# Matmuls on constants in TensorE's waits, in a twelve-layer perceiver kernel

## What is computed

```python
x = x + _L0_xattn_ref(_layernorm(x), ctx_768, ...)   # one head
x = x + _L0_attn_ref(_layernorm(x), ...)             # 16 heads, causal, latent projection
x = x + _L0_ffn_ref(_layernorm(x), ...)              # 8 experts, each picks its top 16 tokens
x = x + _L1_xattn_ref(_layernorm(x), ctx_768, ...)   # 16 heads of 64
x = x + _L1_attn_ref(_layernorm(x), ...)             # 16 heads of 16 + 32
x = x + _L1_ffn_ref(_layernorm(x), ...)              # 16 experts, top 2, capacity 8
x = x + _L2_xattn_ref(_layernorm(x), ctx_768, ...)   # 16 heads of 64
x = x + _L2_attn_ref(_layernorm(x), ...)             # one head, causal
x = x + _L2_ffn_ref(_layernorm(x), ...)              # 8 experts, masks by affinity and rank
x = x + _L3_xattn_ref(_layernorm(x), ctx_768, ...)   # one head
x = x + _L3_attn_ref(_layernorm(x), ...)             # one head
x = x + _L3_ffn_ref(_layernorm(x), ...)              # 64 small two-layer networks
```

```python
aff = num / (x_norm * w_norm[None, None, :] + 1e-09)
cap = jnp.floor(S * jax.nn.sigmoid(aff.mean() - affinity_threshold)).astype(jnp.int32)
...
ranks = jnp.argsort(jnp.argsort(-aff, axis=1), axis=1)
dispatch = tcr * (ranks < cap)
```

## Time and profile before

| | |
|---|---|
| median of 3 runs | 1697.69 us (1694.96 to 1699.32) |
| the profiled execution | 1698.85 us, span 1697.1 us |
| mean granted TensorE clock | 0.881 |
| TensorE matmul busy | 1439.9 us, 85% of the span, 9148 records |
| VectorE, ScalarE, GpSimd busy | 877.0, 644.0, 115.8 us |
| share of the last chain | TensorE 74%, VectorE 14% |

### The profile page before, as it was taken

One profiled execution on the slowest core, in us unless ns is written; L12 is line 12 of the kernel. 1 busy time (PEld: TensorE's weight loads), 2 busy tenths in 40 slices (PEclk: granted clock), 3 DMA queues, 4 the chain that ended last, 5 costly groups with the idle time before them and its releaser, 6 DMA issues.

```text
span 1697.1 us, 22614 instructions
## 1 busy us (share of the span) xinstructions
PE 1439.9 (85%) x9148; PEld 886.4 (52%) x9148; DVE 877.0 (52%) x1631; ACT 644.0 (38%) x890; POOL 115.8 (7%) x76
## 2 busy tenths in 40 slices
PE   5967578899999998786889999999846788886975
PEld 3556367355555556564845555555532555554543
DVE  5545421466566552434246566565266766664434
ACT  4502011355555551110135555555112556453202
POOL 0000000000000000000000000000030434230000
PEclk9975589899999999785789999999965999897985
DMA  5210126255565665001225565556400232230000
GB/s 198 79 50 1 49 99 248 35 107 102 107 106 100 105 109 171 1 0 75 100 44 100 106 106 100 106 106 110 121 25 25 77 103 95 87 126 11 1 0 13
DMA packets 283976, 140.22 MB, mean 83 GB/s; under 512 B 271840, under 2 KB 271840, under 8 KB 277472
## 3 DMA queue, kind: packets, MB, share of 16 engines
q1 hardware_dynamic: 283872, 138.77, 34.0%
HBM read 71.10 MB, written 0.52 MB: 42 GB/s over the span
## 4 chain that ended last, share of the span: by engine, by line
PE 74%; DVE 14%; issue 6%; ACT 3%; POOL 2%; DMA 1%; POOLq 0%; SPq 0%; ACTq 0%; DVEq 0%; PEldq 0%; PEld 0%
PE ps L226 28%; PE ps L1595 5%; PE ps L1559 4%; PE ps L1581 4%; PE ps L1598 3%; PE ps L1582 3%; PE ps L1583 3%; PE ps L1561 3%; PE ps L1560 3%; PE ps L1562 3%; PE ps L1566 2%; PE ps L1522 2%; PE ps L1542 2%; PE ps L1613 2%; PE ps L1619 2%
## 5 line engine op out<-in xcount | busy, mean ns | idle before, releaser
L885 DVE TENSOR_REDUCE wk<-ps 128x1 f32<-128x1024 f32 x128 | 156.8, 1225 | 233.0 <-PE ps L1566 233.0
L545 ACT ACTIVATE wk<-ps,wk 128x1024 f32<-128x1024 f32 x128 | 142.7, 1115 | 237.9 <-DVE wk L885 237.9
L226 PE MATMUL ps<-ring,wk 128*128 128x256 f16 (+2 forms) x1032 | 169.4, 318 | 36.8 <-DVE wk L1411 32.1
L226 PE MATMUL ps<-wk,ring 128*128 128x512 f16 (+4 forms) x896 | 188.2, 364 | 9.7 <-ACT wk L710 2.4
L226 PEld LDWEIGHTS ps<-ring,wk 128*128 128x128 f16 (+2 forms) x1032 | 126.8, 129 | 81.5 <-DVE wk L1411 38.7
L554 ACT ACTIVATE wk<-wk 128x1024 f16<-128x1024 f32 x128 | 146.9, 1148 | 53.6 <-DVE wk L892 53.6
L900 DVE SCALAR_TENSOR_TENSOR wk<-wk 128x1024 f16<-128x1024 f32 x128 | 163.4, 1277 | 2.4 <-ACT wk L554 2.4
L226 PEld LDWEIGHTS ps<-wk,ring 128*128 128x128 f32 (+1 forms) x896 | 110.4, 167 | 64.7 <-issue 26.3
L226 PE MATMUL ps<-wk 16*64 16x64 f32 (+7 forms) x1012 | 89.5, 287 | 25.4 <-DVE wk L1372 11.1
L463 POOL TENSOR_TENSOR rstd<-rstd,cst 128x4 f32<-128x4 f32 x13 | 13.1, 1010 | 1372.4 <-DVE rstd L841 1372.4
L1559 PE MATMUL ps<-ctx_T,ring 128*128 128x512 f16 x256 | 97.7, 382 | 3.6 <-DVE ring L881 3.0
(11 more groups left out here) (293 smaller groups left out, 2322.4 us busy)
## 6 DMA issues: line engine op xcount, KB each, us to landing
ring<-units SPq DMA_DIRECT2D x50, 1024.0 KB, 5.7
ring<-context SPq DMA_DIRECT2D x16, 384.0 KB, 3.9
wk<-context SPq DMA_DIRECT2D x16, 384.0 KB, 3.2
ring<-wk SPq DMA_TRANSPOSE x120, 3.1
ring<-units SPq DMA_DIRECT2D x2, 768.0 KB, 6.5
xn<-wk SPq DMA_TRANSPOSE x64, 3.1
xnT<-wk SPq DMA_TRANSPOSE x64, 3.1
cst<-consts SPq DMA_DIRECT2D x1, 912.5 KB, 5.2
```

Of the source, the lines that this page charges most:

```text
L226: return PE.matmul(out, lhsT, rhs, start=start, stop=stop)
L545: ACTE.activation(WXP[:, t % 2, :], bank(2 * (t % 2), 1024), ACT.Exp, bias=WNM[:, t % 4:t % 4 + 1], accum_out=WRS[:, t % 4:t % 4 + 1]).the ...
L885: DVE.tensor_reduce(WNM[:, t % 4:t % 4 + 1], bank(2 * (t % 2), 1024), X, ALU.max, negate=True).then_inc(xa_max, 1)
```

## The change

A helper `keep_clock(n, b)` on TensorE issues `n` matmuls of fp16 operands, 128 x 128 weights and 512 columns, both read from `cst`, into bank `b`, which nothing reads at that time. It waits for nothing and tells nothing. It is called ahead of every layernorm's transposes, in `self16` ahead of each tile's wait for `sa_P` (12 for the first tile of a half, 5 for the others), in `self1` ahead of the wait for `s1_P`, and at ten places in the routers and in the last layer. In `self16` the wait for `sa_vs` moves from behind the first tile's transposes to ahead of its fillers. There are 522 such matmuls in one execution.

```diff
+            def keep_clock(n, b):
+
+                for _ in range(n):
+                    PE.matmul(ps[:, b, :], cst[:, 0:64].bitcast(F16), cst[:, 0:256].bitcast(F16), start=True, stop=True)
+
-            def layernorm(key):
+            def layernorm(key, spare=7, n=8):
+                keep_clock(n, spare)
                 for i in range(NT):
                     pe.wait_ge(ln_xn, 4 * LN[key] + i + 1)
...
                     def attend(u):
                         t = 8 * k + 4 * h + u
                         ii, j = u // 2, u % 2
+                        if u == 0:
+                            pe.wait_ge(sa_vs, 2 * k + h + 1)
+                        keep_clock(12 if u == 0 else 5, 7)
                         pe.wait_ge(sa_P, t + 1)
...
                         pe.wait_ge(sa_PT, t + 1)
-                        if u == 0:
-                            pe.wait_ge(sa_vs, 2 * k + h + 1)
...
                 ins.then_inc(s1_S, 1)
+                keep_clock(16, 1)
                 pe.wait_ge(s1_P, 1 + k)
...
-            layernorm(0)
+            layernorm(0, n=18)
...
             ins.then_inc(router_logits, 1)
+            keep_clock(8, 7)
             pe.wait_ge(router_d, 1)
             spread_scores(0)
+            keep_clock(44, 7)
             pe.wait_ge(L0f_sel, 1)
...
             ins.then_inc(comb_T, 1)
+            keep_clock(8, 4)
             pe.wait_ge(xin_copied, 4)
...
-            layernorm(3)
+            layernorm(3, n=24)
...
             ins.then_inc(router_logits, 1)
+            keep_clock(14, 7)
             pe.wait_ge(L1f_hot, 1)
...
             mm(bank(3, 64, at=64), C("same"), TU, False, True).then_inc(L1f_cum, 1)
+            keep_clock(16, 7)
             pe.wait_ge(L1f_disp, 1)
...
-            layernorm(6)
+            layernorm(6, spare=2)
...
-            layernorm(8)
+            layernorm(8, spare=3)
...
             ins.then_inc(router_logits, 1)
+            keep_clock(56, 7)
             pe.wait_ge(L2f_sums, 1)
...
             mm(bank(3, 2, at=8), C("ones"), RB_[:, 0:2]).then_inc(L2f_summed, 1)
+            keep_clock(10, 7)
             pe.wait_ge(L2f_mean, 1)
...
+            keep_clock(40, 7)
             pe.wait_ge(L2f_xnl, 1)
             gather(0)
...
-            layernorm("9b")
+            layernorm("9b", n=36)
...
-            layernorm(11)
+            layernorm(11, spare=3)
...
             ins.then_inc(L3f_s, 1)
+            keep_clock(36, 7)
             pe.wait_ge(L3f_acc, 16)
```

## The result

The changed kernel takes 1691.44 us (median of 20 runs, 1669.84 to 1707.87), the one before 1697.28 (20 runs, 1694.37 to 1699.32): 5.8 us less by these medians. The ratio, 0.9928 with the interval 0.9906 to 0.9950, says 12.2 us, because it leaves out the seven slow executions of the changed kernel, those more than 1.5% above its fastest; the median of the other 13 is 1685.99. So 6 to 12 us are gained where 29 were forecast; the time lies inside the range, near its upper end. The profiled execution took 1687.22, span 1685.4, against 1697.1 before: 11.7 us.

A forecast was written before the change was run, and what follows sets the result against it. TensorE's speed, 1.2 instead of 2.4 GHz in low stretches, was taken as the bound. Terms 9 + 14.5 + 6 + 7 + 5 + 1 - 12.3 = 30 us gave 1698.85 - 30 - 1.2 = 1668 us, range 1646 to 1693.

The forecast's parts named there:

- the 56: Third router: 56 fillers ahead of four small matmuls that start a chain push the rest of the program, -12.3 us.
- (c): Rival at the third router: the 56 fillers are hidden, 1656 us; chance 0.06.
- (f): Rival: matmuls on constants don't hold the clock, nothing gained, the 56 cost 24 and the loops 22: 1744 us; chance 0.03.
- The layernorms' share: Layernorms with 8 fillers: 13.0 us saved at full clock, times 0.7, gives 9.
- I take 0.8 and 0.2: Multi-head self-attention half-loops: 0.8 for full clock, 0.2 for low; loops 5 us, with the stages behind 14.5.
- three signs of being wrong: Loops run low (round over 7 us), clock falls after most layernorms, or L1339 no longer waits for GpSimd.
- the first single-head attention with its layernorm: Single-head self-attentions: 16 fillers in a 4.55 us gap, 6.4 times 0.9 gives 6 us; layernorms counted in their 9.
- the last layer: Last layer: 36 fillers in 9.75 us, then eight matmul pairs, half of 4.4 taken; 5 us with the other long gaps.
- One more, for a stretch of expert matmuls that by chance fell low: 1: Expert matmuls: 1 us gained for a stretch that by chance fell to the low clock.
- (a): Likeliest case: clock mostly up in self-attentions, part of the layernorms, the 56 paid: 1648 to 1690 us; chance 0.60.
- (d): Rival: idle left behind fillers, with transposes and copies, still drops the clock at most layernorms: 1680 us; chance 0.12.
- (e): Rival: fillers at the low clock in the multi-head loops, 5.4 us lost per half, 22 in all: 1704; chance 0.09.

The follow-up runs named there:

- e3: Kernel before plus only the 108 fillers of the multi-head self-attentions and the moved wait for sa_vs: 1685.31 us, ratio 0.9936.
- e6: Kernel before plus only the 150 fillers ahead of layernorms: 1681.02 us, ratio 0.9915.
- e4: Kernel before plus only the 56 fillers of the third router: 1710.29 us, ratio 1.0079.
- e1: Changed kernel with the 56 fillers moved behind the first two small matmuls of the third router: 1677.43 us, ratio 0.9878.
- e9: e5 plus 3 fillers in each copy wait of the multi-head loops, between a tile's transposes and its value matmuls: 1659.30 us, ratio 0.9784.
- e7: e3 with fillers that read 16 rows instead of 128, same columns: 1719.64 us, ratio 1.0137.
- e14: A further profile of the changed kernel, nothing edited: 1689.32 us, one run.
- e5: Changed kernel plus 8 and 3 fillers ahead of and within the second feed-forward's experts: 1670.75 us, ratio 0.9849.
- e8: Changed kernel with e1's and e5's edits, 11 fillers per layernorm, 3 in copy waits of layernorms and self-attentions: 1643.71 us, ratio 0.9690.
- e12: e8 plus 3 fillers each in score-spreading waits and ahead of the last cross-attention's and single-head output projections: 1638.69 us, ratio 0.9655.
- e2: Changed kernel without the 108 fillers of the two multi-head self-attentions: 1708.69 us, ratio 1.0072.
- e11: Changed kernel without the 56 fillers: 1680.74 us, ratio 0.9880.
- e10: Kernel before plus only the 8 and 3 fillers at the second feed-forward's experts: 1692.06 us, ratio 0.9965.
- e15: Another further profile of the changed kernel, nothing edited: 1676.46 us, one run.

## Why the prediction was right, and where it was wrong

**The direction and most mechanisms were right.** Matmuls on constants hold the clock (e3, e6); rounds at the full clock are 4.55 us; the 56 push the rest by their whole length, +12.98 us at VectorE's step behind the four small matmuls against the 12.3 forecast, and alone they cost 13.1 (e4). The gap behind them stayed, and moving them gave 14 (e1). Rivals (c) and (f) are out. The layernorms' share up to the first loop came as forecast only on average (3.2 forecast, 4.4 in this execution, 1.5 to 6.3 over four); the second router gave 2.2 as forecast, the first 3.2 for 2.4.

**The step that failed is "I take 0.8 and 0.2"**, the chance of a half-loop being at the full clock, which made 14.5 us of the multi-head attentions. The prices on both sides of it were sound: 24.8 us when all four are up (e9, forecast 25.1), 20.3 lost when all are down and stay so (e7, forecast 22, with nothing gained behind). But in the change 5 of the 16 half-loops of four executions ran at the full clock throughout, none of them in the second attention. There the clock fell at the first round of both halves in all four executions. So the profiled execution got 5.6 + 1.5 = 7.1 where 14.5 were forecast, and the four on average 10.3. A low half also costs less than forecast: with none full throughout, e14 still gained 6.2; in two of its halves the clock rose part-way, and the last five fillers took 1.25 again. The prediction counted the gap of 0.68 us ahead of the value matmuls in the length of the round and asked nothing of it for the clock. With it filled the loops stay up: e9 changes nothing else against e5, and 12 of 12 halves ran at full clock in e8, e9 and e12, against 13 of 32 without.

**Two of the prediction's three signs of being wrong came.** That "the loops run low (round over 7 us)": 7.66 in the second attention. That "the clock falls after most layernorms": after nine of the twelve, and after six of the nine with eight fillers, where the prediction took a share of 0.7 of what full clock would save. The price of that was small: in e6 the clock is low behind ten of the twelve, and still its layernorms gave 11.1 us where 11.4 were forecast. Fillers ahead of the transposes keep these at 1.41 us and let the low stretch begin later. So this term came out right in size, in this one profile, though the clock did what the prediction counted as a sign of being wrong.

**Four smaller terms were mis-sized,** by the profiled execution: the first single-head attention with its layernorm gave 0.9 of some 3.4 (the part of the 6 and the 9 that falls there); the third router's spreading and gather 1.9 of 2.7; the last layer 1.5 of 2.6; and two places that the prediction had at nothing cost time: the third feed-forward's experts 2.6 and the last cross-attention's output projection 4.2, whose groups of four take 2.08 us in the change where they took 1.13. The last was at 2.4 GHz before, without any filler. (The prediction takes the 1.13 of the earlier trace rows for the last self-attention's; it is this cross-attention's.) In e3, whose fillers all lie 800 us ahead of it, it is low as well, so the fillers did not lower it by their own work. It is low in all four executions of the change and in e1, e2, e3, e5, e8, e9 and e11, and at full clock in e4, e6, e7, e10 and e12; what decides is not shown, nor why the experts take 2.6 more. Together 7.4 + 2.5 + 0.8 + 1.1 + 2.6 + 4.2 = 18.6, less what the start and the first router gave above forecast (2.0), plus 0.7 for the 56: 17.3 of the 18.3 us that lie between 30 and 11.7.

**"One more, for a stretch of expert matmuls that by chance fell low: 1"** had the right place and no idea of its size. Those three groups took 41.8 (e2), 26.4 (the change) and 22.2 us (e5). The term should have been a range of 5 us of gain to 15 of loss. The four executions of the change itself agree there; the other values came with other sets of fillers.

**Of the rivals** the 1691 lies just above the upper end of (a) and between the 1680 of (d) and the 1704 of (e). (d) is right on what the clock does and wrong on its price: the clock falls behind most layernorms, with 1.10 us of gap, 1.41 of transposes and 0.79 of copy behind the fillers, but by e6 the layernorms were not where the gain went. The Trainium skill, TensorE: Matmul & The Clock Gate, Part 4, says that transpose-mode work doesn't count as busy for the clock. The trace agrees at nine of twelve layernorms; at the first one with eight fillers the clock stayed up in two of four executions and fell in two, over the same gap, transposes and copy, and no run parts the transposes from the waits around them. The largest part of what is missing is that of (e), in part of the halves.

**The spread was not foreseen.** The kernel before spreads over 5 us, the change over 38. The four profiles show where 13 of these come from: the clock at the first layernorms and in the loops falls in one execution and not in another. It seems to take the 108 and the others together, since e3 and e2, which have one of the two, spread over 5 and 4 us in five runs each; why is not shown. The Trainium skill, TensorE: Matmul & The Clock Gate, Part 1, says that the number of slow matmuls at a kernel's start differs from run to run, and puts the penalty of that start at under 1% of a typical kernel. Here 38 of 1691 us are 2.2%, in a kernel whose clock falls and rises again at many places.

**What stays open.** No execution above 1689 us was profiled, so where the slowest ones lose up to 19 us more is not shown. The experts at 1.2 GHz throughout, as in e2, would be 15 of them, and would also explain why the eleven fillers of e5 are worth 5.6 us at their stage and 13 to 21 in the time; but none of the four profiles has them so. What lets the clock fall at one of two equal places and not at the other is open throughout.

## What to carry to other kernels

Ask of each stretch whether it can raise the clock by itself; one that can't (here groups of 64 columns, matmuls of 1 to 48 rows, loops with short gaps) may run at either, which is worth its whole length at half speed, and belongs into a forecast as two cases for each such stretch, not as a share. Put fillers at its entry and in its smallest waits, with all 128 rows, and never ahead of a wait that is already met on the path: look at which instruction starts the chain across the gap, and put them behind it. Profile such a kernel several times before believing one trace.

## What the runs showed of the hardware

- Fillers that read 16 rows don't hold the clock where fillers of 128 rows do: 1719.64 against 1685.31 us (e7, e3; the values read change with the rows).
- 192 matmuls of 128 rows and 64 columns of fp32, 42 us with one gap of 0.90, did not raise the clock from 1.2 GHz (e2). Entered at 2.4 GHz, 128 of them ran 14.84 us at it; the third group fell behind a gap of 0.90 us in which TensorE waited for VectorE, in nine of eleven profiles, and stayed up with 0.81 us of fillers in that gap in five of five (e5, e8, e9, e10, e12).
- TensorE busy for 20.40 of 20.40 us with matmuls of 1, 128 and 48 rows in turn ran at a granted clock of 0.51 (e12, 710.8 to 731.2).
- Behind eight fillers, 1.10 us of gap, 1.41 of transposes and 0.78 of copy, the clock fell at the same layernorm in two executions of one program and stayed up in two (four matmuls in 3.42 and 3.49 us, or 1.98). With eleven fillers ahead and three in the copy wait it was low behind one and two of twelve layernorms (e8, e12), against seven to nine.
- The same program gives loops at either clock in different executions (e14, e15), though its instructions and their order are fixed.
- The gain of one set of fillers depends on the others: by the ratios, the 108 in the attentions gave 11 us alone (e3) and 24 on top of the others (e2 against the change), the eleven at the experts 6 alone (e10) and 13 on top of the change (e5).
